# A six-stage decoder kernel on one core: identity products that fill TensorE's waits are dropped, except at the start

## What is computed

```
x = x + mamba(layernorm(x))            # in-projection 512 -> 2320, chunked state space with 16 heads, gate, out-projection
x = x + memory_attention(layernorm(x), ctx, mask)   # softmax(x ctx^T / sqrt(512)) ctx, one head
x = x + routed_ffn(layernorm(x))       # the top 128 of 512 tokens of each row go through 512 -> 2048 (gelu) -> 512
x = x + attention(layernorm(x))        # causal grouped-query attention, 16 heads of 32, over the axis of 4
x = x + quantized_matmul(layernorm(x), ctx)         # blocks of 128 rounded to fp8
x = x + bit_ffn(layernorm(x))          # rounded activations, weights of -1, 0 and 1, 512 -> 1408 -> 512
```

## Time and profile before

| | |
|---|---|
| median of 3 runs | 1037.58 us |
| the profiled execution | 1038.19 us, its span 1036.3 us |
| mean granted TensorE clock | 0.995 |
| TensorE (PE) busy | 1004.3 us, 97% |
| its weight loads (PEld) | 746.9 us, 72% |
| VectorE (DVE) busy | 825.9 us, 80% |
| ScalarE (ACT) busy | 661.1 us, 64% |
| GpSimd (POOL) busy | 444.7 us, 43% |
| chain that ended last, by engine | PE 73%, DVE 12%, ACT 5%, issue 4%, POOL 4% |
| the same by line | PE L471 56%, L555 5%, L943 3%, L479 3%, L485 1% |

### The profile page before, as it was taken

The page is one execution under the profiler, slowest core; times in us unless marked ns, Lnnn a source line. Parts: engine busy times, 40 slices in busy tenths (PEclk is TensorE's granted clock), DMA queues, the critical chain, the costliest instruction groups (busy, mean ns, idle before and its releaser), DMA issues.

```text
span 1036.3 us, 15017 instructions
## 1 busy us (share of the span) xinstructions
PE 1004.3 (97%) x4949; PEld 746.9 (72%) x4949; DVE 825.9 (80%) x1751; ACT 661.1 (64%) x1252; POOL 444.7 (43%) x655
## 2 busy tenths in 40 slices
PE   8999999999999999899999999998999999999998
PEld 7787788778877887665766887867766766666544
DVE  6898878787788787648898778677878988979875
ACT  5755555555555554356666567755489999898874
POOL 3435224422432233327888442016554645635520
PEclk9999999999999999899999999999999999999999
DMA  8453333333333422263100164310001111112124
GB/s 298 183 153 106 98 113 102 102 92 113 102 102 102 113 92 82 94 250 155 41 1 1 32 240 141 138 41 1 1 11 26 28 25 34 24 21 54 35 59 139
DMA packets 100860, 91.90 MB, mean 89 GB/s; under 512 B 79152, under 2 KB 80432, under 8 KB 96432
## 3 DMA queue, kind: packets, MB, share of 16 engines
q1 hardware_dynamic: 100784, 90.96, 28.0%
HBM read 56.69 MB, written 15.60 MB: 70 GB/s over the span
## 4 chain that ended last, share of the span: by engine, by line
PE 73%; DVE 12%; ACT 5%; issue 4%; POOL 4%; DMA 1%; SPq 0%; DVEq 0%; ACTq 0%; POOLq 0%
PE bank L471 56%; PE bank L555 5%; PE bank L943 3%; PE bank L479 3%; PE bank L546 1%; PE bank L566 1%; PE bank L485 1%; DMA land<-win_in 1%; DVE ctx_lo L1308 1%; DVE wgt L1066 1%; POOL prod L2633 1%; DVE spare L1347 1%; PE bank L855 1%; DVE half_lo L1421 0%; POOL y L2422 0%
## 5 line engine op out<-in xcount | busy, mean ns | idle before, releaser
L471 PE MATMUL bank<-win_hi,a_uT_hi 128*128 128x512 f32 (+1 forms) x320 | 126.1, 394 | 3.3 <-DVE win_lo L1023 2.5
L471 PE MATMUL bank<-win_lo,a_uT_hi 128*128 128x512 f32 (+1 forms) x320 | 120.5, 377 | 0.0
L471 PE MATMUL bank<-win_hi,a_uT_lo 128*128 128x512 f32 (+1 forms) x320 | 120.0, 375 | 0.0
L2422 POOL TENSOR_TENSOR y<-y,off 128x512 f32<-128x512 f32 x24 | 37.9, 1580 | 91.5 <-DVE off L1085 91.5
L471 PEld LDWEIGHTS bank<-win_hi,a_uT_hi 128*128 128x128 f32 x320 | 60.6, 189 | 17.0 <-DVE win_lo L1023 3.6
L471 PEld LDWEIGHTS bank<-win_hi,a_uT_lo 128*128 128x128 f32 x320 | 60.7, 190 | 11.3
L1066 DVE TENSOR_SCALAR wgt<-cum_all,neg 128x128 f32<-128x128 f32 x256 | 67.9, 328 | 0.4 <-DMA cum_all<-cum_rows 0.4
L1801 ACT ACTIVATE zs<-y 128x1024 uint16<-128x1024 uint16 x30 | 31.7, 1057 | 56.6 <-DVE y L1100 56.6
L471 PEld LDWEIGHTS bank<-win_lo,a_uT_hi 128*128 128x128 f32 x320 | 60.8, 190 | 9.5 <-issue 0.2
L471 PE MATMUL bank<-f,fqT_next 128*128 128x512 fp8e4 (+1 forms) x312 | 64.0, 362 | 0.0
L555 PEld LDWEIGHTS bank<-xs,wgt 128*128 128x128 f32 x512 | 61.3, 196 | 1.9 <-issue 0.4
(11 more groups left out here) (348 smaller groups left out, 3009.3 us busy)
## 6 DMA issues: line engine op xcount, KB each, us to landing
cum_all<-cum_rows SPq DMA_DIRECT2D x16, 1024.0 KB, 4.7
wchunk<-w_in SPq DMA_DIRECT2D x32, 256.0 KB, 5.6
y_rows<-zs SPq DMA_DIRECT2D x30, 256.0 KB, 2.0
stage<-f_in SPq DMA_DIRECT2D x3, 1408.0 KB, 6.0
x<-x_in SPq DMA_DIRECT2D x16, 256.0 KB, 5.5
land<-win_in SPq DMA_DIRECT2D x4, 1024.0 KB, 8.4
wq<-ctxT_in SPq DMA_DIRECT2D x4, 1024.0 KB, 6.6
out<-x SPq DMA_DIRECT2D x16, 256.0 KB, 2.6
```

The source lines that it names most:

```text
L471: made = e.matmul(bank, a, b, start=start and n == 0, stop=stop and n == len(pairs) - 1)
L2422: e.tensor_tensor(y[m % 2][:, cols], y[m % 2][:, cols], off[:], ALU.add).then_inc(sig("y_off"), 1)
```

## The change

All calls of keep_busy go, but for the one in turn_un(0), which runs while the first row of x is loaded. The waits and the order of everything else stay. In ffn_down(8) the claim of a bank goes too.

```diff
@@ project
                 bank = banks.claim(w, (("proj0", "proj_x", "proj_x", "proj_z", "proj_z")[n], i, n), *let_go)
-                if i == 0 and n in (0, 2):
-                    keep_busy(bank, (12, 0, 4)[n])
@@ pair
-                if m == 1:
-                    keep_busy(bank, 8)
@@ recall
-                if i in (6, 10, 14):
-                    keep_busy(bank, 6)
@@ spread_weights
-                if b == BATCH - 1:
-                    keep_busy(bank, 3)
@@ positions
-                keep_busy(bank, 5 if b == BATCH - 1 else 3)
@@ early_up
-                if f == 0:
-                    keep_busy(bank, 7)
@@ ffn_down
-                if f == KF // 2:
-                    keep_busy(banks.claim(w, ("busy", f), "up_done", f + 1), 6)
@@ scatter
-                if n == 0:
-                    keep_busy(bank, 5)
@@ attend_out
-                if n in (0, 2, 3, 4):
-                    keep_busy(bank, 5)
@@ turn_eu
-                if n in (0, 1, NT - 3):
-                    keep_busy(bank, 6)
```

## The result

The kernel after takes 1041.83 us (median of 20 runs, 1039.34 to 1048.38), the one before 1037.25 us beside it (20 runs); the ratio is 1.0041, with a 95% interval of 1.0025 to 1.0056. I had said 1036.9 us and a range up to 1041.6. The profiled execution of after took 1045.67 us, 7.5 more than that of before.

A forecast was written before the change was run, and what follows sets the result against it. Most of the span was taken as paced by TensorE, the rest by short loops over ScalarE and VectorE. From 1037.9 us, less 4.2 gain, plus 3.2 for two clock falls: 1036.9 us, range 1033.4 to 1041.6.

The forecast's parts named there:

- The gain, 4.2: Time won where removed products delayed ready work, summed place by place: 4.2 us, ends about 1 and about 7.3.
- the routing of the first batch: Products before positions (3) and recall (6): gain 1.1 us, ends 0.4 and 1.7, limited by when b_u is ready.
- the banks' rotation: Middle of the feed-forward layer: the dropped bank claim shifts later claims; costed at 0, at worst taking back the 1.3 us.
- the wait of 2 us that I foretold at 537: Sign in the second routing batch: a wait for pT_lo of about 2 us stands where products stood.
- The price of the clock, 3.2: Two falls of TensorE's clock to half, 1.6 us each, expected among the gaps at 535, 584 to 594, 694 and 974 us.
- Before the first projection ... Gain 0: The 12 products there gain 0: TensorE idles another 0.75 us after them, until VectorE has made a_uT_lo.
- Before the third projection ... Gain 0: The 4 products there (0.9 us) gain 0: the running sum already waits 0.94 us for dt, and that wait grows.
- I take 0 and keep 1.2: A clock fall at the start slows the first projection by up to 1.2 us; costed at 0, 1.2 kept as possible.
- No transfer is near: In the places that gain, work moved earlier needs only weights and chunks already there, so no transfer limits it.
- Slower: the clock falls in nearly every gap: Rival: four falls in the gaps and one at the start, 3.4 us more, 1041.3 us; chance 0.21.
- The gains are taken up downstream: Rival: routing and attention wait for ScalarE and VectorE, gain only 1.5 us with two falls, 1039.6 us; chance 0.13.
- the stretch from 490 to 527: Sign for the routing: it gets shorter by about 1 us; if not, VectorE or ScalarE paced the routing.

The follow-up runs named there:

- e10: Kernel before with all 124 dropped products made 4 x 4 in place of 128 x 128, instructions kept; 1037.73 us, ratio 1.0000.
- e12: Kernel before without the 40 products in front of ready work, plus 24 products of 4 x 4 before the first turn_u; 1033.86 us, ratio 0.9963.
- e9: Kernel after with the 16 start products put back as 4 x 4 ones (64 instructions); 1038.01 us, ratio 1.0001 to before.
- g1: Kernel before with the 16 start products replaced by 4 of 512 columns (16 instructions); 1040.14 us, ratio 1.0022.
- e11: Kernel after with 16 products of 4 x 4 before the first turn_u, in the wait at 424 us; 1039.22 us, ratio 1.0012 to before.
- g2: Kernel after with 8 products of 4 x 4 before the first projection (32 instructions); 1038.61 us, ratio 1.0013 to before.
- e2: Kernel before without the 84 products that fill waits, the 40 in front of ready work kept; 1043.60 us, ratio 1.0072.
- e1: Kernel before without the 40 products in front of ready or nearly ready work, the other 84 kept; 1033.82 us, ratio 0.9976.
- e7: Kernel before without only the 16 products in front of the first and third projection; 1042.69 us, ratio 1.0039.
- e8: Kernel before without the 40 products in front of ready work, plus 12 full ones before the first turn_u; 1035.65 us, ratio 0.9976.

## Why the prediction was wrong, by its steps

**The sum itself held.** It said 4.2 us of gain less 3.2 for the clock, 1.0 to the good. e10 is nearest to what it summed (columns gone, instructions kept), and shows 0 with an interval of 1.6 us to either side. Part of that is luck, as the next two steps say.

**The gain, 4.2.** e12 removes what pays and has its packets well placed: 0.37%, 3.8 us. By place, from the starts of the same products in before and after (in brackets what I had): pair(1) 0.4 (0.4); the routing of the first batch 0.5 (1.1), since 1.2 of 1.7 us went again in waits of 0.35 to 0.45 for ScalarE and VectorE; of the second 1.2 (0); of the third 0.1 (0.1); the feed-forward layer 1.3 (1.3), with nothing taken by the banks' rotation; scatter 0.5 (0.45); turn_eu 1.25 (0.85). The sum is about 5.2. In the second batch I had read the wait of 0.17 us for pT_lo as fixed; but pT_lo came earlier too, and the wait of 2 us that I foretold at 537 is not there.

**The price of the clock, 3.2.** That two of the gaps bring a fall, the count behind the 3.2, was my estimate, and no run shows it; in its place the runs show this. e10 against e12 is 0.37%, 3.8 us, of which up to 1.0 is the time of the 40 thin products themselves (a quarter of 4.2): 2.8 to 3.8. The size came out, by another count: by the mean clock of the runs, e10 spent 14 to 15 us more at half clock than e12, as much as four of the stretches of 3.4 us, so about 0.8 us each, where I had two at 1.6. Each costs 1.5 to 1.7 us at once, near what I wrote, but not all lie "where TensorE paces": at 592 and 701 us 1.1 and 1.5 came back at the next wait, which leaves 0.4 and 0.2. The gap at 535 never opened, and 643 and 763 were not on my list. The clock fell more with the cover gone (eight half-clock windows of after above, two in before), but not behind every long gap: behind 717.54 us (1.55 idle) there was none.

**The step that failed: "Before the first projection ... Gain 0", "Before the third projection ... Gain 0", and, for the clock at the start, "I take 0 and keep 1.2".** TensorE's own waits there behaved as I wrote (0.75 became 3.43, 0.94 became 1.75). What I never asked is what else 64 instructions are. They have a share in when the next 16 KB of TensorE's program is fetched (first packet at 17.78 us with them, at 28.15 without), and without them the fetch met the 8 KB write, which landed after 3.43 us and not 1.37. That their count matters is shown without the cover: putting 64 thin instructions back gave 0.40% (e9), and taking 48 away with the columns kept cost 0.22% (g1). After against e10 is 0.41%, 4.2 us: as large as the whole loss, and with the thin products' 1.0 us as large as my error, give or take 2 us. How it divides is open. The trace of after has 2.1 us at 41.77, 1.5 at half clock behind it, 1.5 at 642.80 and 1.5 behind that, but the medians of e11 and g2 put the larger part behind the start, and that part is not traced to a fetch. "No transfer is near" looked at the transfers that the moved work needs, not at what else shares the DMA engines.

**The rivals.** "Slower: the clock falls in nearly every gap" named 1041.3, near the result, and the profiled execution has its count of falls. But e10, with the same gaps and the instructions kept, isn't slower: two of the falls in after (43 and 643 us) come behind late operands, not behind gaps of removed products, and two others cost next to nothing. Its number is near by luck. "The gains are taken up downstream", 1039.6, shows in the first batch of routing alone.

**The signs.** L485 has 28 records, oT_lo's waits are 1.5 to 2.1, d_u's 3.0, and TensorE is busy for 15 us less, not 20, since the other products take longer in the half-clock stretches (37 us in after, 10 in before; a 512-column product takes 0.63 us there, at 43.14, and 0.40 at full clock, at 41.05 in before). Two signs failed: the wait of 2 us for pT_lo at 537 is missing, and the stretch from 490 to 527 is shorter by only 0.5, which by my own words means that VectorE or ScalarE took the rest. The feed-forward stretch should have been 1.3 shorter; it gained that, lost 3.1 to the chunk and the clock, and came out 1.7 longer.

What a 16 KB instruction packet cost shows at the write: in the nine traces in which one met it, it landed 1.06 to 2.06 us later than the 1.37 us of before.

## What to carry to other kernels

The 64 instructions of the start products, whose results nobody reads, had a share in the place of the fetches behind them: without them the first moved by 10 us, from 17.78 to 28.15. Look in the DMA view for the instruction queue's packets beside small transfers on the critical path, before and after. To tell what filler gives by its activity from what it gives by its count, replace it by the thinnest one with the same instructions, and by fewer and wider ones with the same columns. Cover paid here where the operand behind it was late (without those 84 products e2 took 0.72% more). The 40 in front of ready work, 9.0 us of TensorE's time at 0.112 a record, cost 2.5 us (0.24%, e1) to 3.8 (0.37%, e12).

## What the runs showed that I had not expected

- The 8 KB write of cum_rows landed after 1.37 to 1.39 us alone (seven traces) and after 2.43 to 3.43 with a 16 KB instruction packet beside it (nine). One of its 16 pieces then ended 0.04 to 0.08 us behind the packet.
- The wait of 2.09 us at 41.77 in after was not caught up in 390 us of work with TensorE nearly full (361 of 363 us busy from 53 to 416): with the 1.5 us of the half-clock stretch behind it, the first transposes of b_u start 3.4 us later (428.01, before 424.58). In g1 a wait of 1.27 us at 41.13 had such a stretch behind it too, in e7 one of 1.29 at 41.23 had none.
- With cover in the wait near 424 us (e8) the half-clock stretch came at 418.4 us and not at 425. In e9, with none there, it came at 418.5, so it is not shown that the cover moved it.
- Time lost in a half-clock stretch was hardly a loss at one place: 1.5 of 1.7 us at 701 us in after came back at the next wait for VectorE.
